# A mixture-of-experts kernel whose first layer hands over its output in two parts, with the residual in the weights

## What is computed

```python
# layer 0: a linear layer and 8 LoRA adapters of rank 16, weighted per batch by cond_8
out  = einsum('btc,oc->bto', x, W_base) + b_base
h    = einsum('btc,erc->bter', x, As)
lora = einsum('bter,eor,be->bto', h, Bs, cond_8)
x1   = x + out + lora * 2.0
# layer 1: the two experts of 8 that cond_8 ranks first, and a shared expert
def mlp(x, g, u, d): return einsum('bsi,ih->bsh', gelu(x @ g) * (x @ u), d)   # I = 512
result = x1 + sum over the two experts e of b: w[b, e] * mlp(x1[b], expert e) + mlp(x1, shared expert)
```

## Time and profile before

| | us |
|---|---|
| median of 3 runs | 134.96 (134.84 to 135.22) |
| the profiled execution | 135.5 |
| its span, first to last instruction | 133.8 |
| TensorE busy | 127.2 (95%) |
| VectorE / ScalarE / GpSimd busy | 88.7 / 70.9 / 60.2 |

### The profile page before, as it was taken

How to read it: one execution, slowest core, us unless ns; L and a number is a source line. 1 busy time by engine, 2 the same in 40 slices (tenths; PEclk the granted TensorE clock), 3 DMA queues, 4 the chain that set the end, 5 groups by cost and what they waited for, 6 DMA issues and landing times.

```text
span 133.8 us, 3280 instructions
## 1 busy us (share of the span) xinstructions
PE 127.2 (95%) x869; PEld 114.2 (85%) x869; DVE 88.7 (66%) x172; ACT 70.9 (53%) x134; POOL 60.2 (45%) x110
## 2 busy tenths in 40 slices
PE   6899999999999989996999999999999999999991
PEld 6658787878878869995999999999989999989991
DVE  2668978779977888533376658656855686756732
ACT  3432867976876766120466485657554755711110
POOL 5209384497777644632064543554255504610000
DMA  3898878798000185599345686558799940013822
GB/s 51 245 335 290 287 197 300 227 308 247 12 2 0 39 266 170 157 394 409 144 174 218 238 316 240 193 201 313 260 316 322 347 167 0 0 41 121 248 85 61
DMA packets 14526, 26.56 MB, mean 199 GB/s; under 512 B 2225, under 2 KB 7601, under 8 KB 12977
## 3 DMA queue, kind: packets, MB, share of 16 engines
q1 hardware_dynamic: 14192, 26.35, 58.8%
q10 hardware_dynamic: 320, 0.07, 0.2%
HBM read 12.52 MB, written 1.31 MB: 103 GB/s over the span
## 4 chain that ended last, share of the span: by engine, by line
PE 78%; DVEq 6%; DVE 4%; issue 4%; DMA 3%; ACT 2%; SPq 0%; ACTq 0%
PE bank L999 8%; PE bank L1036 7%; PE bank L1035 7%; PE bank L1034 7%; PE bank L946 5%; PE bank L948 5%; PE bank L947 5%; DVEq L232 5%; PE bank L1016 5%; PE bank L1056 4%; PE bank L962 3%; PE bank L1058 3%; PE bank L1057 3%; PE bank L871 3%; PE bank L964 3%
## 5 line engine op out<-in xcount | busy, mean ns | idle before, releaser
L533 ACT ACTIVATE work<-bank 128x512 f32<-128x512 f32 x48 | 28.7, 598 | 43.0 <-PE bank L1036 18.3
L697 DVE TENSOR_TENSOR bank<-bank,work 128x512 f32<-128x512 f32 x40 | 27.9, 697 | 23.2 <-PE bank L1036 12.5
L714 DVE TENSOR_TENSOR hT_lo<-bank,hT_hi 128x512 fp32r<-128x512 f32 x40 | 27.3, 682 | 1.7 <-issue 0.8
L1034 PE MATMUL bank<-xp,wst 128*128 128x256 f32 x96 | 27.2, 284 | 0.0
L1035 PE MATMUL bank<-xp,wst 128*128 128x256 f32 x96 | 27.2, 283 | 0.0
L1036 PE MATMUL bank<-xp,wst 128*128 128x256 f32 x96 | 27.1, 283 | 0.0
L463 POOL TENSOR_TENSOR wstd<-wexd,wstd 128x512 fp32r<-128x512 f32 x12 | 15.5, 1295 | 23.8 <-ACT wstd L575 23.8
L542 ACT CAST hT_hi<-bank 128x512 fp32r<-128x512 f32 x40 | 23.3, 582 | 2.4 <-DVE bank L697 1.3
L1035 PEld LDWEIGHTS bank<-xp,wst 128*128 128x128 f32 x96 | 18.4, 192 | 0.0
L1036 PEld LDWEIGHTS bank<-xp,wst 128*128 128x128 f32 x96 | 18.4, 192 | 0.0
L1034 PEld LDWEIGHTS bank<-xp,wst 128*128 128x128 f32 x96 | 18.4, 192 | 0.0
(11 more groups left out here) (146 smaller groups left out, 212.7 us busy)
## 6 DMA issues: line engine op xcount, KB each, us to landing
wst<-wex SPq DMA_DIRECT2D x12, 1024.0 KB, 5.0
raw_ex<-n_L_cond_skill_gate_dram SPq DMA_DIRECT2D x8, 256.0 KB, 3.3
raw_ex<-in_L_cond_skill_up_dram SPq DMA_DIRECT2D x8, 256.0 KB, 4.2
sst<-n_L_cond_skill_gate_dram SPq DMA_DIRECT2D x8, 256.0 KB, 3.4
sst<-in_L_cond_skill_up_dram SPq DMA_DIRECT2D x8, 256.0 KB, 4.2
xn<-in_x_dram SPq DMA_DIRECT2D x4, 256.0 KB, 4.6
out_dram<-xT SPq DMA_DIRECT2D x4, 256.0 KB, 2.7
sst<-_L_cond_shared_gate_dram SPq DMA_DIRECT2D x1, 256.0 KB, 4.6
```

The source lines that it names most:

```text
L533: act.activation(gelu_sb[q], gate_ps[q][:, :], ACT.Gelu_apprx_tanh).then_inc(gelu_done, 1)
L697: dve.tensor_tensor(up_ps[u][:, :], up_ps[u][:, :], gelu_sb[q], ALU.mult).then_inc(h_done, 1)
L714: dve.tensor_tensor(hT_lo[:, q, :], up_ps[u][:, :], f32(hT_hi[:, q, :]), ALU.subtract).then_inc(lo_done, 1)
L1034: pe.matmul(of_c, w_hi, x_hi, start=True, stop=False)
```

## The change

- The residual goes into the weights: `wT` is W_base transposed plus the identity matrix (the same one VectorE operation, now with a second operand), so that F(g) gives x1 less the bias.
- `x1_hi(g)` is written for all four groups by ScalarE, straight from PSUM with the bias added (an activation, Identity). `x1_lo(g)` is written for all four by VectorE, from PSUM, bias and `x1_hi`. VectorE's `first_layer` is gone.
- x1 itself is not needed before the sums of the shared expert: GpSimd's new `x1_whole(g)` adds the two parts into `total`, and `sum_group(g)` waits for it.
- `sB` has 4 places; groups 2 and 3 are scaled by GpSimd, behind `setup_sb` 2 (that is `bT`).
- ScalarE loads the table of gelu before `copy_xT(2)`.
- VectorE takes `w_eff(2)` before the first split. `x1lo_ready` stands where `x1_ready`, `x1lo_first` and `x1lo_later` stood.

TensorE's instructions and their order are the same. GpSimd's new `x1_whole(3)` stands behind `up_lo(1, 2)`, where `x1_split(3)` stood ahead of it.

```diff
+            pool.wait_ge(setup_sb, 2)
+            for g in range(2, NG):
+                pool.tensor_tensor(sB[:, g, :, :],
+                                   bT[:, :].rearrange("p (a o) -> p a o", a=1).to_broadcast([P, GB, H]),
+                                   lora_s[:, g * GB:(g + 1) * GB].rearrange("p (b a) -> p b a", a=1)
+                                   .to_broadcast([P, GB, H]), ALU.mult).then_inc(sB_later, 1)
...
-            def x1_split(g):
-                if g >= 2:
-                    pool.wait_ge(x1_ready, g + 1)
-                    pool.tensor_copy(x1_hi(g), xn[:, g * GB:(g + 1) * GB, :]).then_inc(x1hi_ready, 1)
-                pool.wait_ge(x1hi_ready, g + 1)
-                pool.tensor_tensor(x1_lo(g), xn[...], f32(x1_hi(g)), ALU.subtract).then_inc(x1lo_later, 1)
+            def x1_whole(g):
+                pool.wait_ge(x1lo_ready, g + 1)
+                pool.tensor_tensor(total[...], f32(x1_hi(g)), f32(x1_lo(g)), ALU.add).then_inc(x1_ready, 1)
...
-            x1_split(1)
-            pool.wait_ge(x1_ready, NG)
+            x1_whole(0)
+            pool.wait_ge(x1_ps, NG)
             pool.memset(base[:, :, :], 0.0).then_inc(base_zero, 1)
...
-            x1_split(2)
+            x1_whole(1)
             up_lo(0, 1)
-            x1_split(3)
+            x1_whole(2)
             up_lo(1, 2)
+            x1_whole(3)
...
             def split_x1_hi(g):
-                act.wait_ge(x1_ready, g + 1)
-                act.copy(x1_hi(g), xn[:, g * GB:(g + 1) * GB, :]).then_inc(x1hi_ready, 1)
+                act.wait_ge(x1_ps, g + 1)
+                act.activation(x1_hi(g), bank[4 + g][...], ACT.Identity, bias=bias[:, 0:1]).then_inc(x1hi_ready, 1)
...
+            act.wait_ge(exp_done, 1)
+            act.activation(rt[:, 24:25], rt[:, 8:9], ACT.Gelu_apprx_tanh).then_inc(gelu_table, 1)
             copy_xT(2)
+            act.wait_ge(ld_bias, 16)
             split_x1_hi(0)
...
-            act.activation(rt[:, 24:25], rt[:, 8:9], ACT.Gelu_apprx_tanh).then_inc(gelu_table, 1)
+            split_x1_hi(2)
+            split_x1_hi(3)
...
-            def first_layer(g):
-                dve.wait_ge(x1_ps, g + 1)
-                dve.wait_ge(xT_ready, g + 1)
-                dve.scalar_tensor_tensor(xn[...], bank[4 + g][...], bias[:, 0:1], xT[...], ALU.add, ALU.add
-                                         ).then_inc(x1_ready, 1)
+            def split_x1_lo(g):
+                dve.wait_ge(x1hi_ready, g + 1)
+                dve.scalar_tensor_tensor(x1_lo(g), bank[4 + g][...], bias[:, 0:1], f32(x1_hi(g)),
+                                         ALU.add, ALU.subtract).then_inc(x1lo_ready, 1)
...
-            dve.tensor_copy(wT[:, :], bank[6][:, 0:H]).then_inc(setup_sb, 1)
+            dve.tensor_tensor(wT[:, :], bank[6][:, 0:H], ident[:, :], ALU.add).then_inc(setup_sb, 1)
...
                 dve.wait_ge(down_done, NC * g + NC)
+                dve.wait_ge(x1_ready, g + 1)
```

More of the change, by code:

```diff
@@ L108, in lora_then_top2_moe @@
         hT_hi = sb("hT_hi", [P, 2, I], F32R)
-        with nc.sbuf_tensor("sB", [P, 2, GB, H], F32) as sB:
+        with nc.sbuf_tensor("sB", [P, NG, GB, H], F32) as sB:
             pass
@@ L159, in lora_then_top2_moe @@
         sB_ready = sem("sB_ready")
+        sB_later = sem("sB_later")
         xT_ps = sem("xT_ps")
@@ L166, in lora_then_top2_moe @@
         x1hi_ready = sem("x1hi_ready")
-        x1lo_first = sem("x1lo_first")
-        x1lo_later = sem("x1lo_later")
+        x1lo_ready = sem("x1lo_ready")
         sh_hi = sem("sh_hi")
@@ L357, in _ @@
             pool.tensor_tensor(wshd[:, 1, :, :], raw_shd[:, :, :], f32(wshd[:, 0, :, :]), ALU.subtract).then_inc(sh_dlo, 1)
-            def x1_split(g):
-                if g >= 2:
-                    pool.wait_ge(x1_ready, g + 1)
-                    pool.tensor_copy(x1_hi(g), xn[:, g * GB:(g + 1) * GB, :]).then_inc(x1hi_ready, 1)
-                pool.wait_ge(x1hi_ready, g + 1)
-                pool.tensor_tensor(x1_lo(g), xn[:, g * GB:(g + 1) * GB, :], f32(x1_hi(g)),
-                                   ALU.subtract).then_inc(x1lo_later, 1)
+            def x1_whole(g):
+                pool.wait_ge(x1lo_ready, g + 1)
+                pool.tensor_tensor(total[:, g * GB:(g + 1) * GB, :], f32(x1_hi(g)), f32(x1_lo(g)), ALU.add
+                                   ).then_inc(x1_ready, 1)
             def up_lo(e, after):
@@ L466, in _ @@
             pool.wait_ge(lists_ready, 2)
-            pool.wait_ge(x1lo_first, 1)
-            pool.wait_ge(x1lo_later, NG - 1)
+            pool.wait_ge(x1lo_ready, NG)
             for s in range(NBUF):
@@ L507, in split_x1_hi @@
             def split_x1_hi(g):
-                act.wait_ge(x1_ready, g + 1)
-                act.copy(x1_hi(g), xn[:, g * GB:(g + 1) * GB, :]).then_inc(x1hi_ready, 1)
+                act.wait_ge(x1_ps, g + 1)
+                act.activation(x1_hi(g), bank[4 + g][:, :].rearrange("p (b s) -> p b s", b=GB), ACT.Identity,
+                               bias=bias[:, 0:1]).then_inc(x1hi_ready, 1)
             act.wait_ge(sort_mm, 1)
@@ L637, in scale_B @@
             def scale_B(g, bT=bT):
-                if g >= 2:
-                    dve.wait_ge(delta_ps, g - 1)
-                dve.tensor_tensor(sB[:, g % 2, :, :],
+                dve.tensor_tensor(sB[:, g, :, :],
                                   bT[:, :].rearrange("p (a o) -> p a o", a=1).to_broadcast([P, GB, H]),
@@ L652, in w_eff @@
                                   ALU.add).then_inc(weff_ready, 1)
-            def first_layer(g):
-                dve.wait_ge(x1_ps, g + 1)
-                dve.wait_ge(xT_ready, g + 1)
-                dve.scalar_tensor_tensor(xn[:, g * GB:(g + 1) * GB, :],
-                                         bank[4 + g][:, :].rearrange("p (b s) -> p b s", b=GB), bias[:, 0:1],
-                                         xT[:, g * GB:(g + 1) * GB, :], ALU.add, ALU.add).then_inc(x1_ready, 1)
+            def split_x1_lo(g):
+                dve.wait_ge(x1hi_ready, g + 1)
+                dve.scalar_tensor_tensor(x1_lo(g), bank[4 + g][:, :].rearrange("p (b s) -> p b s", b=GB), bias[:, 0:1],
+                                         f32(x1_hi(g)), ALU.add, ALU.subtract).then_inc(x1lo_ready, 1)
             dve.wait_ge(setup_ps, 1)
@@ L670, in _ @@
             dve.wait_ge(setup_ps, 3)
-            dve.tensor_copy(wT[:, :], bank[6][:, 0:H]).then_inc(setup_sb, 1)
+            dve.wait_ge(consts, 1)
+            dve.tensor_tensor(wT[:, :], bank[6][:, 0:H], ident[:, :], ALU.add).then_inc(setup_sb, 1)
             router_weights()
@@ L674, in _ @@
             w_eff(0)
-            scale_B(2)
             w_eff(1)
-            scale_B(3)
+            w_eff(2)
             dve.wait_ge(ld_bias, 16)
[L679 to L684, removed]
+            split_x1_lo(0)
             w_eff(3)
@@ L689, in _ @@
                               ALU.subtract).then_inc(sh_lo, 1)
-            first_layer(2)
-            first_layer(3)
+            for g in range(1, NG):
+                split_x1_lo(g)
             def gated(t, q, u):
@@ L868, in delta_w @@
             def delta_w(g):
-                pe.wait_ge(sB_ready, g + 1)
-                pe.matmul(bank[g][:, :], a_sb[:, :], sB[:, g % 2, :, :].rearrange("p b o -> p (b o)"),
+                if g < 2:
+                    pe.wait_ge(sB_ready, g + 1)
+                else:
+                    pe.wait_ge(sB_later, g - 1)
+                pe.matmul(bank[g][:, :], a_sb[:, :], sB[:, g, :, :].rearrange("p b o -> p (b o)"),
                           start=True, stop=True).then_inc(delta_ps, 1)
@@ L892, in sort_starts @@
                 pe.wait_ge(sort_step, S_PAR)
-                pe.wait_ge(x1_ready, NG)
+                pe.wait_ge(x1lo_ready, NG)
                 pe.matmul(start_ps[0:B, 0:24], half[:, :], upick[:, :, :].rearrange("p a e -> p (a e)"),
@@ L940, in gate_up_shared @@
                     elif first == U_HI and t == 2:
-                        pe.wait_ge(x1_ready, 1)
+                        pe.wait_ge(x1lo_ready, 1)
                     elif first == U_HI:
@@ L955, in down_shared @@
                     if isinstance(g, int) and g == 0:
-                        pe.wait_ge(x1_ready, 2)
+                        pe.wait_ge(x1lo_ready, 2)
                         pe.wait_ge(sh_dlo, 1)
@@ L1078, in _ @@
             pe.wait_ge(sh_lo, 1)
-            pe.wait_ge(x1lo_first, 1)
+            pe.wait_ge(x1lo_ready, 1)
             shared_group(0)
-            pe.wait_ge(x1lo_later, 1)
+            pe.wait_ge(x1lo_ready, 2)
             shared_group(1)
             for g in range(2, NG):
-                pe.wait_ge(x1lo_later, g)
+                pe.wait_ge(x1lo_ready, g + 1)
                 shared_group(g)
```

## The result

The changed kernel takes **136.28 us** (median of 8 runs, 135.86 to 136.94) against 135.11 us for the kernel before in the same series: a ratio of 1.009, with a 95% interval of 1.0063 to 1.0116. Forecast was 134.68. The profiled execution took 136.94 us with a span of 135.3 us; that of before took 135.5 with 133.8.

The account below looks back on a forecast made before the run. TensorE, busy 127.2 of 133.8 us, was taken as the bound; only its 0.28 us idle ahead of F3 could go, all else costing 0. Span 133.8 - 0.28 = 133.5, median 134.68 us, range 134.3 to 135.3.

Parts of the forecast that it names:

- GpSimd's list work: GpSimd's operations up to the last `rows`, ahead of the lists' matmul: end near 39.3 to 39.4, cost 0, 0.2 us spare.
- the start of the shared expert: TensorE's first load there wants 16.16 and waits for L688, which may take up to 1.13 us, ending 16.1: just fits.
- The wait ahead of F3: Prologue: TensorE idles 0.28 us until VectorE's `w_eff(3)` is done; the change lets F3 start at 15.28, removing the gap.
- No more than that can go: Gain ahead of F3 limited to 0.28 to 0.30 us: F2's loads end at 15.28, `xT` of group 3 at 15.21.
- The low part of the up weights: VectorE's L688 (`sh_lo`) beside GpSimd's `x1_whole(0)`: 0.68 us alone, up to 1.13, ending at 16.1.
- rival 1: The lists come late: TensorE waits 0.2 us (134.9, chance 0.12), or the matmul is 0.57 later (135.5, chance 0.08).
- GpSimd's two scale_B: Prologue scaling of groups 2 and 3 on GpSimd: ends at 7.9 us, before D3 is loaded at 13.01; cost 0.
- Rival 2: `x1_whole(0)` and VectorE's L688, L663 slow one another; first load or step 2 waits 0.1 to 0.3 us: 134.8 to 135.0; chance 0.12.
- two of the signs that I had named for being wrong: Signs included L688 over 1.13 us with a gap behind it, and the lists' matmul at 40.0 or later.
- Rival 4: Prologue: ScalarE's high part takes over 0.9 us instead of 0.65, VectorE still reaches `w_eff(3)` late: 134.96; chance 0.06.
- rival 3: Late-stage waits not hanging on TensorE alone fall away (134.2 to 134.5) or come (134.9 to 135.1); chance 0.14.

Follow-up runs that it names:

- whole0_later: Changed kernel with `x1_whole(0)` moved from beside VectorE's L688 to behind `pos_ke`, where GpSimd idles: 135.96 us, ratio 1.0068.
- sB_on_dve: Changed kernel with all four `x1_whole` moved to GpSimd's idle times or behind its list work, and `scale_B(2)`, `scale_B(3)` back on VectorE: 134.45 us, ratio 0.9928.
- after_sB_dve: Changed kernel with one part undone, `scale_B(2)` and `scale_B(3)` on VectorE again: 135.42 us, ratio 1.0014.
- lists_first: Changed kernel with `x1_whole(3)` moved behind `up_lo(4, 5)`, that is behind GpSimd's list work: 135.21 us, ratio 1.001.

## Why the prediction was wrong

The steps that failed are two terms that the sum put at nothing: GpSimd's list work ("Cost 0, with 0.2 us to spare"), which cost 1.13 us, and the start of the shared expert ("That just fits"), which cost the 0.24 us that the change brought. Of the 1.60 us between 134.68 and 136.28, the first makes 1.13 and the missing gain 0.28; the kernel before itself came out 0.15 slower in this series than the 134.96 that I had started from.

**The wait ahead of F3: right.** The gap closed and brought 0.24 us (1.89 against 2.13 in `whole0_later`), for a forecast of 0.28. "No more than that can go" held for this order of events only: it took one execution's TensorE for all.

**The low part of the up weights: the price failed.** I had the collision, priced L688 at up to 1.13 us and found that it just fits. It took 1.38 and cost all of the gain. I took the two rows with a collision as a bound, though the operations overlapped only in part in them. They already fit what the later rows show: whoever starts second takes its own time plus the rest of the first, less some 0.13 us. L641 has 0.68 + (11.31 - 10.85) - 0.12 = 1.02. By it my own schedule (GpSimd until 15.65, L688 from 15.0) gives 0.68 + 0.65 - 0.13 = 1.20 and an end at 16.2, already too late for 16.16. The rest is that `x1_whole(0)` ran until 16.21, with L688 from 15.37: 0.68 + 0.84 - 0.14 = 1.38.

**GpSimd's list work: rival 1, with a price that its worst case did not reach.** It had 0.08 for a full 0.57 us; it was 1.13. I counted 1.25 us for `x1_whole(3)`, a stall of L418 that vanishes (it did), and arrived at 0.2 us to spare. Against that the trace of the changed kernel shows, on GpSimd:

```profile
32.31 1.29 POOL L376 TENSOR_TENSOR wex<-raw_ex,wex 128x512 fp32r<-128x512 f32 x1 [2.20 <-DVE wex L719]
33.56 1.78 POOL L369 TENSOR_TENSOR xn<-x1s 128x512 f32<-128x512 f32 x1
35.30 0.18 POOL L423 TENSOR_TENSOR lp<-left_rank 16x1 f32<-16x1 f32 x1
...
39.53 0.97 POOL L444 TENSOR_SCALAR rows<-iota,lp,top_idxf 16x32 f32<-16x32 f32 x1
```

against VectorE's splits:

```profile
33.50 0.68 DVE L719 TENSOR_TENSOR wex<-raw_ex,wex 128x512 fp32r<-128x512 f32 x1
...
39.62 0.71 DVE L719 TENSOR_TENSOR wex<-raw_ex,wex 128x512 fp32r<-128x512 f32 x1
```

`x1_whole(3)` took 0.50 more, since VectorE's L719 was first this time, by 0.06 us. A write of `rows` took 0.51 more, since the chain had been pushed into the next L719 (it was the one held, though its row starts 0.09 us ahead). And the chain began 0.43 late with step 6's product, which no row of before could show. 0.50 + 0.51 + 0.43 = 1.44 against 0.2 to spare: a wait of 1.2, and 1.13 are seen. I had let two stalls of the old position vanish and not asked which new ones the new position meets. My own times had one: L719 at 33.13 - 0.28 = 32.85 falls into `x1_whole(3)` from 32.45 to 33.7, so that one of the two had to be held. The 0.43 I could not have known.

**GpSimd's two scale_B: "cost 0" was wrong.** The working looked only at who reads `sB`. It did not ask who else wants GpSimd's access to SBUF from 5.3 to 7.9 us. The earlier trace rows had the warning, L418 at 0.67 us for 16 numbers. Its price is a floor under F0 at 9.37 us, which binds only when TensorE is fast early, up to 0.8 us (8.59 in `sB_on_dve`). That `sB_on_dve` is 0.6 us faster in the median fits it, but no row shows how often the floor binds.

**The rivals.** Rival 2 came true on top of rival 1, and so did two of the signs that I had named for being wrong: L688 over 1.13 us, and the lists' matmul behind 40.0. Rival 4 did not come true: ScalarE's high part took 0.69 us. Of rival 3 nothing was seen: from the lists to the end both kernels take 93.8 or 93.9 us. I gave one case per rival and added none of them up; two that both rest on the same neighbour should have been priced together.

## What to carry to other kernels

In this kernel, work that was moved to an idle engine had to be priced by what it excludes, not only by who waits for its result. For such a move, list VectorE's operations in GpSimd's new window and the other way round, and take the wait of whoever starts second as the whole rest of the first. Here, an operation of 1.3 us ahead of a chain of small dependent operations with under 1 us of slack was a loss; behind the chain, or in an idle time ahead of it, it cost nothing. And a wait read in one profile belongs to that execution's order of events: with the engine in front of it a microsecond faster, another pair of operations collided, and 0.28 us became 1.05. The version with `x1_whole` in GpSimd's idle times, the scaling on VectorE and two more matmuls of zeros takes 133.98 us, 1.1% less than the kernel before.

## What the runs showed of the hardware

- Two operations on VectorE and GpSimd, each with two inputs in SBUF, ran one after the other: the second took its own time plus the rest of the first, less 0.13 us or so (1.38 for 0.68 and 1.45 for 0.69 on VectorE, 1.78 for 1.28 on GpSimd). Where both start within 0.1 us of one another, the rows don't tell beforehand who is held: `x1_whole(3)` was, 0.06 behind L719, but so was a write of `rows`, 0.09 ahead of it. Small ones are stopped as well: 0.95 for 0.15 (L635), 0.97 for 0.46 (`rows`). VectorE's operations that read PSUM and one SBUF tile were not longer beside GpSimd: the split of x1 took 0.75 in `after_sB_dve`, and `w_eff(3)` 0.68 at 14.77 beside `x1_whole(0)` in the changed kernel. The Trainium skill ("GPSIMD Engine Reference", section "Key points") names contention between GpSimd and VectorE's instructions with two SBUF inputs. The rows agree, and they show its size and that it goes both ways.
- ScalarE's Identity from PSUM with a bias took 0.69 us at its first (2.10 for three in a row), over the 0.65 that I took. The estimate by the Trainium skill ("ScalarE: Activation LUTs", section "What ACT_TABLE_LOAD costs") is 707 ns for one with a pointer as bias, and the row agrees. It cost nothing, as forecast.
- VectorE lost 0.43 us at one place of its program, or not, by two instructions more or fewer ahead of it (1.12 us of idle time in seven profiles, 0.69 in seven). The cause is open.
- TensorE became fast at another time in each execution: the record of full clock begins at 10.64 and 9.52 us in two executions of the changed kernel, and at 8.11 in `lists_first`, which has the same prologue. With two small matmuls in a gap it begins at 5.78 to 6.84, and D0 took 1.02 to 1.23 us in place of 1.79 to 1.92. Rows that lie ahead of the record print a granted clock of 1.00 at half the pace.
